# Value products of causal attention: one float32 matmul becomes three passes on high and low halves, two blocks late

## The chip, the cores and the metric

The kernel runs on one core of one Trainium2 chip. The metric is the device time of one execution in microseconds (us), smaller is better. The core has a matrix engine (TensorE, in the profile PE, its weight loads PEld), VectorE (DVE), ScalarE (ACT), GpSimd (POOL) and SyncE (SP), each with its own instruction queue worked off in order; they wait for each other on semaphores.

## The reference

The program is a two-layer network on an input `x` of 2 x 1024 x 256. Layer 0 is a Mamba block and a mixture of experts, layer 1 an attention with three heads over all tokens, then a causal attention, and a second mixture of experts. The change is in the causal attention, 16 query heads and 4 key heads of width 128:

```python
q = (x @ wq).reshape(b, s, H, HD)          # H = 16, KV = 4, HD = 128, s = 1024
k = (x @ wk).reshape(b, s, KV, HD)
v = (x @ wv).reshape(b, s, KV, HD)
q, k = apply_rope(q, cos, sin), apply_rope(k, cos, sin)
scores = jnp.einsum('bqhd,bkhd->bhqk', q, k) / np.sqrt(HD)
scores = jnp.where(causal[None, None], scores, jnp.finfo(scores.dtype).min)
probs = jax.nn.softmax(scores, axis=-1)
out = jnp.einsum('bhqk,bkhd->bqhd', probs, v).reshape(b, s, H * HD)
return out @ wo
```

## The kernel before

The causal attention is the function `attn2`. It works through eight units, `u` = 0 to 7: one key head of one batch with its `REP` = 4 query heads. In a unit the queries are cut into `TB` = 8 rows of blocks, 128 queries each, worked in descending order, row 7 first; row `i` has `i + 1` key blocks `j`. The function `schedule()` writes one list, `todo`, of tokens, and every engine goes through this list and does its part of each token, so the order of the tokens is the order in each queue:

- `score` (u, i, h): TensorE multiplies queries of row i and head h with the keys in three passes. Queries and keys are kept as a high half (rounded to the fast float32r format) and a low half (the rest), and `THREE` names the passes (high x high, high x low, low x high). VectorE takes the maximum (`reduce_max`, then `nb`), ScalarE the exponential, and the normalization by the reciprocal of the sum is GpSimd's for heads 0 to 2 and VectorE's for head 3 (`normal`).
- `turn` (u, i, j): TensorE transposes the four heads' probabilities of block j into one bank of its accumulation memory (PSUM), 4 or 5 in turn; ScalarE copies it into `eT`.
- `value` (u, i, j): TensorE adds `v[:, j]` times `eT` into the row's accumulator (bank 6 or 7), in float32. It comes one `turn` after its own.
- `out` (u, i): the finished row, copied by ScalarE into `ao`, is multiplied by `wo`; VectorE adds it to `hs`. It takes a bank of the same pair 4 and 5, and is put ahead of the second product of the next row.
- `project` (u, n), five in a unit for the next unit (the key and four heads): in row 4 before blocks 0, 2 and 4, in row 3 before block 2, in row 2 before block 1. TensorE makes it in 12 passes; VectorE applies the rotation (L1867 to L1869) and for the key subtracts its high half (L1873); GpSimd adds the parts (L1890) and makes the low half of the queries (L1895). The rotation of query head n waits for the low half of head n - 2.
- `values` (u): the projection of `v`, copied by ScalarE (L1976). In unit 0 `chores` puts the second batch's normalization on VectorE, one piece at each `turn`; unit 3 has four pieces more.

Scores, projections and `values` share banks 0 to 3 as they come (`unit_free` waits for whoever used the bank before); `turn` and `out` share banks 4 and 5 (`ring_free` waits for the entry before the last one).

Of the kernel before, what the change touches and what calls it, by code (L numbers as in the profile page):

```python
# [7 lines left out]
P = 128  # L8
F32 = mybir.dt.float32
# [1554 lines left out]
def attn2(nc, g, hs, norm_w, wq, wk, wv, wo):  # L1564
# [8 lines left out]
    with ctx:  # L1573
# [8 lines left out]
        WPIECE, WPIECES = 256, WC // 256  # L1582
        wo_s = sb("wo", [P, 2, REP, D])
        cos, sin = sb("cos", [P, L]), sb("sin", [P, L])
        mask_f, mask, ident_b = sb("mask_f", [P, P]), sb("mask", [P, P], BF16), sb("ident_b", [P, P], BF16)
        HI, LO = 0, 1
        ER = 4
        hT, wh, qT, kT = ([
            sb(n + half, shape, F32R) for half in ("hi", "lo")] for n, shape in (
            ("hT", [P, KC, L]), ("wh", [P, KC, WC]), ("qT", [P, REP, L]), ("kT", [P, L])))  # L1590
        v, eT = sb("v", [P, TB, HD]), sb("eT", [P, ER, REP * P])
        THREE = ((HI, HI), (HI, LO), (LO, HI))
        e = sb("e", [P, 2, REP, L])
        side = sb("side", [P, REP, 5 * P])
        ao = sb("ao", [P, 2, REP, P])
        mx, nb, sm, rc = (sb(n, [P, TB * REP]) for n in ("mx", "nb", "sm", "rc"))
        d_x = nc.dram_tensor("a2_dx", [B * L, D], F32, kind="Internal").ap()
        names = ("in", "own", "xn", "tr", "hT", "hlow", "whigh", "wlow", "cst", "unit", "w", "rot", "sum", "high", "rope", "rope_k",
                 "v", "nb", "e", "rc", "en", "en_last", "xout", "xin", "spare", "wo_in",
                 "tp", "eT", "o", "ao", "wo", "hs")  # L1600
        s = {n: sem(n) for n in names}
        block = ctx.enter_context(nc.Block())
        U = B * KV
# [21 lines left out]
        def schedule():  # L1625
# [9 lines left out]
            def turn(u, i, j):  # L1635
                put("turn", u, i, j)
                waiting.append((u, i, j))
                if len(waiting) > 1:
                    value(*waiting.pop(0))

            ahead = {7: [(p, 6, h) for h, p in enumerate((0, 1, 2, 3))] + [(p, 3, h) for h, p in enumerate((4, 5, 6, 7))],
# [71 lines left out]
        @block.sync  # L1713
        def _(sp):
            loads = [(nwb[:, :], norm_w.rearrange("(a n) -> a n", a=1).to_broadcast([P, D])),
                     (cos[:, :], g.d["cos"]), (sin[:, :], g.d["sin"]),
                     (mask_f[:, :], g.d["mask"])]
            sp.dma_start(d_x.rearrange("(j p) d -> p j d", p=P), x[:, :, :]).then_inc(s["xout"], 16)
            for u in range(U):
                kv = u % KV  # L1720
                if u > 0:
                    sp.wait_ge(s["wlow"], u * WPIECES)
                sp.dma_start(w_s[:, :, 0:REP * HD], wq.rearrange("(k p) n -> p k n", p=P)[:, :, kv * (REP * HD):(kv + 1) * (REP * HD)]).then_inc(s["w"], 16)
                sp.dma_start(w_s[:, :, REP * HD:(REP + 1) * HD], wk.rearrange("(k p) n -> p k n", p=P)[:, :, kv * HD:(kv + 1) * HD]).then_inc(s["w"], 16)
# [12 lines left out]

        @block.vector
        def _(dve):
# [59 lines left out]
            inverse(0, 2)  # L1799
            dve.wait_ge(s["in"], 64)  # L1800
            scaled(0, 0, TB)
            dve.tensor_copy(mask[:, :], mask_f[:, :])
            dve.tensor_copy(ident_b[:, :], ident[:, :]).then_inc(s["cst"], 1)

            def chores(u):
# [11 lines left out]
                    c += [lambda q=q: scaled(1, 2 * q, 2) for q in range(4)]  # L1817
                return c

            late, extra = [], []  # L1820

            def normal(u, i, h):
                q = i * REP + h
# [5 lines left out]
                    dve.tensor_scalar(probs(i, h), probs(i, h), rc[:, q:q + 1], None, ALU.mult).then_inc(s["en_last"], 1)  # L1829

            for what, u, i, h in todo:
                if what == "score":
                    n = unit[what, u, i, h]
                    q = i * REP + h
                    dve.wait_ge(s["unit"], done[what, u, i, h])
                    own(dve.reduce_max(mx[:, q:q + 1], pair(n, (i + 1) * P), AX_X))  # L1836
                    dve.tensor_scalar(nb[:, q:q + 1], mx[:, q:q + 1], -SCALE, None, ALU.mult).then_inc(s["nb"], 1)  # L1837
                    if late:
                        normal(*late.pop(0))
                    late.append((u, i, h))  # L1840
# [1 line left out]
                elif what == "turn":  # L1842
# [76 lines left out]
        def _(act):  # L1919
# [36 lines left out]
            for n, (what, u, i, h) in enumerate(todo):  # L1956
                if what == "turn":
                    k = turned[u, i, h]
                    act.wait_ge(s["tp"], k + 1)
                    act.activation(eT[:, k % ER, :], ps[:, bank[what, u, i, h], :], ACT.Copy).then_inc(s["eT"], 1)  # L1960
                    if u == 0 and (i, h) == (7, 5):
                        root(1, 3)
                    if u == 0 and (i, h) == (4, 3):
                        root(1, 4)
# [8 lines left out]
                    act.activation(hT[HI][:, int(i), :], pair(unit[what, u, i, h]), ACT.Copy).then_inc(s["hT"], 1)  # L1973
                elif what == "values":
                    act.wait_ge(s["unit"], done[what, u, i, h])
                    act.activation(flat(v[:, :, :]), pair(unit[what, u, i, h]), ACT.Copy).then_inc(s["v"], 1)  # L1976
# [14 lines left out]
        def _(pe):  # L1991
            pe.wait_ge(s["cst"], 1)

            def unit_free(token):

                for what, u, i, h in earlier[token]:
# [2 lines left out]
                    elif what == "project":  # L1999
                        pe.wait_ge(s["rot"], u * NPROJ + i + 1)  # L2000
                    elif what == "values":
                        pe.wait_ge(s["v"], u + 1)
                    else:
                        pe.wait_ge(s["hlow"], 2 * u + i + 1)

            def ring_free(t):

                r = ring_at[t]
                if r >= 2:
                    what, u, i, j = ring[r - 2]  # L2010
                    if what == "turn":
                        pe.wait_ge(s["eT"], turned[u, i, j] + 1)
                    else:
                        pe.wait_ge(s["hs"], outs[u, i] + 1)

            for token in todo:
# [53 lines left out]
                    tr.then_inc(s["tp"], 1)  # L2070
                elif what == "value":
                    k = turned[u, i, j]
                    pe.wait_ge(s["eT"], k + 1)
                    if j == 0:
                        if i == TB - 1:
                            pe.wait_ge(s["v"], u + 1)
                        if rows[u, i] > 1:
                            pe.wait_ge(s["ao"], rows[u, i] - 1)
                    mm = pe.matmul(ps[:, 6 + rows[u, i] % 2, :], v[:, j, :], eT[:, k % ER, :], start=(j == 0), stop=(j == i))  # L2079
                    if j == i:  # L2080
                        mm.then_inc(s["o"], 1)
                elif what == "out":
# [96 lines left out]
```

## Time and profile before

| | |
|---|---|
| median of 3 runs | 2725.68 us (2723.99 to 2726.79) |
| profiled execution | 2727.46 us, its span 2725.7 us |
| TensorE busy (PE) | 2422.0 us, 89% of the span |
| VectorE busy (DVE) | 1428.0 us, 52% |
| ScalarE busy (ACT) | 1131.9 us, 42% |
| GpSimd busy (POOL) | 1135.4 us, 42% |
| `attn2` | about 1484 to 2414 us of the span |

A busy share is an average over stages. What counts for the change is the stretch of `attn2`: which engine is full there, and where it waits. Matmuls overlap in the trace, since each is shown from its start to its last result; the distance between two starts tells what one occupies. A row of a timeline gives start, duration, engine, line, operation, and in brackets how long the engine had been idle and who ended it.

### The profile page before, as it was taken

What the parts mean: (1) busy time and instruction counts of PE and PEld (TensorE: products, weight loads), DVE (VectorE), ACT (ScalarE), POOL (GpSimd) and SP (SyncE); (2) the same over time, 40 slices, a digit from 0 to 9 for tenths busy, and PEclk for the clock granted to TensorE, in tenths of its full rate; (3) what the DMA queues carried; (4) which work ended last, traced back from release to release, by engine and by line L of the source; (5) the groups of instructions that cost most, each with busy time, mean ns of one, the idle gap of its engine ahead of it and who ended that gap; (6) DMA issues with size and microseconds to landing.
All of it is one profiled execution on the core that took longest, in us unless ns stands there. A gap on an engine that the chain in (4) does not pass through costs nothing. (4 is left out here: it accounts for less than half of the span.)

```text
span 2725.7 us, 34445 instructions
## 1 busy us (share of the span) xinstructions
PE 2422.0 (89%) x12334; PEld 1805.0 (66%) x12334; DVE 1428.0 (52%) x2528; ACT 1131.9 (42%) x1920; POOL 1135.4 (42%) x666
## 2 busy tenths in 40 slices
PE   6959999968999949969994799999999999968997
PEld 2349999946777638848862567776677776734554
DVE  6568888772222235434426575555555555453332
ACT  3557777621111124324421446455464554531221
POOL 0449999602333204322422454444444445303443
PEclk8969999989999969989986899999999999988999
DMA  6282351255112120000002000000000000036222
GB/s 236 86 318 56 132 233 63 86 163 186 32 32 33 27 95 1 1 1 1 1 1 88 1 12 20 9 12 8 13 20 9 12 8 18 15 102 190 45 45 61
DMA packets 107469, 168.22 MB, mean 62 GB/s; under 512 B 30468, under 2 KB 76166, under 8 KB 105096
## 3 DMA queue, kind: packets, MB, share of 16 engines
q1 hardware_dynamic: 92328, 145.22, 15.2%
q0 software_dynamic: 14976, 20.78, 4.6%
q8 instruction: 106, 1.74, 0.3%
q14 instruction: 59, 0.48, 0.1%
HBM read 115.81 MB, written 52.32 MB: 62 GB/s over the span
## 5 line engine op out<-in xcount | busy, mean ns | idle before, releaser
L670 POOL TENSOR_TENSOR mb_dbx<-mb_ud,mb_bb 128x1024 f32<-128x1024 f32 x128 | 302.0, 2363 | 58.1 <-DVE mb_h L528 42.4
L528 DVE TENSOR_TENSOR_SCAN mb_h<-ps,mb_dbx 128x1024 f32<-128x1024 f32 x128 | 292.2, 2289 | 49.5 <-ACT ps L640 42.2
L2079 PE MATMUL ps<-a_eT,a_v 128*128 128x512 f32 x576 | 298.3, 600 | 1.3 <-ACT a_eT L1960 1.3
L1908 POOL TENSOR_TENSOR a_e<-a_e,a_rc 128x1024 f32<-128x1024 f32 (+5 forms) x144 | 187.9, 1310 | 266.1 <-DVE a_rc L1826 265.7
L1836 DVE TENSOR_REDUCE a_mx<-ps 128x1 f32<-128x1024 f32 (+7 forms) x256 | 192.8, 753 | 199.8 <-PE ps L2060 199.4
L968 POOL DMA_INDIRECT e_acc<-e_hid,e_ids x78 | 123.6, 1585 | 371.4 <-DVE e_hid L1264 364.0
L1960 ACT ACTIVATE a_eT<-ps 128x512 f32<-128x512 f32 x288 | 171.1, 594 | 250.1 <-PE ps L2069 249.3
L772 PE MATMUL ps<-mb_dg,mb_hts 128*128 128x128 f32 x2048 | 251.9, 277 | 0.4
L772 PEld LDWEIGHTS ps<-mb_dg,mb_hts 128*128 128x128 f32 x2048 | 240.6, 193 | 1.9 <-issue 1.9
L1558 POOL TENSOR_TENSOR a_elo<-a_e,a_ehi 128x1024 fp32r<-128x1024 f32 x48 | 120.6, 2513 | 264.9 <-ACT a_ehi L1482 264.9
L2057 PE MATMUL ps<-a_kThi,a_qThi 128*128 128x512 f32 (+3 forms) x384 | 206.4, 537 | 21.6 <-DVE a_e L1869 9.8
L1250 DVE COPY e_work<-ps 128x256 f32<-128x256 f32 x78 | 33.1, 425 | 357.0 <-PE ps L1083 357.0
L1942 ACT ACTIVATE a_e<-ps,a_nb 128x1024 f32<-128x1024 f32 (+5 forms) x192 | 156.1, 813 | 87.2 <-DVE a_nb L1837 74.0
L1114 PE MATMUL ps<-e_wd,e_work 128*128 (+1 forms) x780 | 189.0, 384 | 1.9 <-ACT e_work L1013 1.9
L1095 PE MATMUL ps<-e_wg,e_work 128*128 x468 | 178.2, 518 | 5.0 <-DVE e_work L1250 1.4
L649 ACT ACTIVATE mb_hts<-ps 128x512 f32<-128x512 f32 x256 | 139.2, 595 | 95.2 <-PE ps L757 95.2
L1007 ACT ACTIVATE e_hid<-ps 128x688 f32<-128x688 f32 (+1 forms) x78 | 52.3, 670 | 300.6 <-PE ps L1095 300.6
L1095 PE MATMUL ps<-e_wu,e_work 128*128 x468 | 171.1, 502 | 0.0
L2069 PE MATMUL ps<-ident,a_e 128*128 128x128 f32 x992 | 151.3, 275 | 18.4 <-DVE hs L1883 16.0
L757 PE MATMUL ps<-ident,mb_h 128*128 128x128 f32 x1024 | 135.6, 276 | 32.9 <-DVE mb_h L528 32.8
L1114 PEld LDWEIGHTS ps<-e_wd,e_work 128*128 128x128 f32 (+1 forms) x780 | 138.9, 190 | 30.0 <-issue 15.7
L954 POOL DMA_INDIRECT e_xin<-e_rows,e_ids x78 | 77.0, 987 | 190.3 <-DVE e_ids L1239 166.6
(343 smaller groups left out, 5293.0 us busy)
## 6 DMA issues: line engine op xcount, KB each, us to landing
mb_bb<-mb_db_rows SPq DMA_DIRECT2D x16, 1024.0 KB, 12.8
mb_ddiag<-mb_dg SPq DMA_DIRECT2D x1, 8192.0 KB, 22.3
mb_dg<-mb_ddiag SPq DMA_DIRECT2D x8, 1024.0 KB, 14.4
e_wg<-in_g SPq DMA_DIRECT2D x8, 688.0 KB, 10.4
e_wu<-in_u SPq DMA_DIRECT2D x8, 688.0 KB, 11.1
e_wd<-in_d SPq DMA_DIRECT2D x8, 640.0 KB, 10.6
mb_dxa<-mb_bb SPq DMA_DIRECT2D x8, 512.0 KB, 2.6
mb_dz<-mb_xz SPq DMA_DIRECT2D x8, 512.0 KB, 2.9
```

The costliest lines, as they stand in the source:

```text
L528: dve.tensor_tensor_scan(h[:, at % 2, :], pair(at % 2), dbx[:, at % 2, :], 0.0, ALU.mult, ALU.add).then_inc(s_h, 1)
L670: pool.tensor_tensor(dbx[:, at % 2, :], ud[:, kk % 2, 0, :], bb[:, n, :], ALU.mult).then_inc(s_dbx, 1)
L772: mm = pe.matmul(ps[:, 6 + half, q * P:(q + 1) * P], hts[:, at % 2, c:c + P], dg[:, n, c:c + P], start=(n == 0 and q == 0), stop=(n == NS ...
L1095: mm = pe.matmul(ps[:, b0 + a, 0:FN], xT[:, i % 2, k * P:(k + 1) * P], w[:, ds(e), k, a * FN:(a + 1) * FN].rearrange("p a n -> p (a n)"), ...
L1114: mm = pe.matmul(ps[:, 6, 0:D], hT[0:n, i % 2, c * P:(c + 1) * P], wd[0:n, ds(e), c, :].rearrange("p a n -> p (a n)"), start=(c == 0), sto ...
L1836: own(dve.reduce_max(mx[:, q:q + 1], pair(n, (i + 1) * P), AX_X))
L1908: pool.tensor_tensor(probs(i, h), probs(i, h), rc[:, q:q + 1].to_broadcast([P, (i + 1) * P]), ALU.mult).then_inc(s["en"], 1)
L1942: act.activation(probs(i, h), pair(n, (i + 1) * P), ACT.Exp, bias=nb[:, q:q + 1], scale=SCALE, accum_out=sm[:, q:q + 1]).then_inc(s["e"], 1)
L1960: act.activation(eT[:, k % ER, :], ps[:, bank[what, u, i, h], :], ACT.Copy).then_inc(s["eT"], 1)
L2057: mm = pe.matmul(ps[:, o + t, 0:c1 - c0], qT[x_][:, j, i * P:(i + 1) * P], kT[y_][:, c0:c1], start=(x_ == y_), stop=(x_ == LO and not last))
L2069: tr = pe.transpose(ps[:, bank[token], h * P:(h + 1) * P], probs(i, h, j * P, (j + 1) * P), ident[:, :])
L2079: mm = pe.matmul(ps[:, 6 + rows[u, i] % 2, :], v[:, j, :], eT[:, k % ER, :], start=(j == 0), stop=(j == i))
```

## The change

The value product is made like the scores, in three passes on high and low halves of `v` and of `eT`. ScalarE's copies now write the high halves `eT[HI]` and `v[HI]` in float32r; VectorE subtracts them from what stands in PSUM and writes the low halves. For `eT` that is the new function `low`, done as VectorE's first work of the token that follows the `turn`. Semaphores `eTlow` and `vlow` take the place of `eT` and `v` where TensorE waits: for a value product, and for the reuse of a bank. The product stands two turns behind its own instead of one. To make room `eT` has three slots instead of four, `mask_f` lies in `side`, and `mx` keeps two rows' worth.

```diff
-        ER = 4
+        ER = 3
-        v, eT = sb("v", [P, TB, HD]), sb("eT", [P, ER, REP * P])
+        v, eT = ([sb(n + half, shape, F32R) for half in ("hi", "lo")] for n, shape in (("v", [P, TB, HD]), ("eT", [P, ER, REP * P])))
...
+        mask_f = side[:, 0, 0:P]
...
-        mx, nb, sm, rc = (sb(n, [P, TB * REP]) for n in ("mx", "nb", "sm", "rc"))
+        nb, sm, rc = (sb(n, [P, TB * REP]) for n in ("nb", "sm", "rc"))
+        mx = sb("mx", [P, 2 * REP])
...
-                if len(waiting) > 1:
+                if len(waiting) > 2:
                     value(*waiting.pop(0))
...
+            def low(u, i, j):
+                k = turned[u, i, j]
+                dve.wait_ge(s["eT"], k + 1)
+                dve.tensor_tensor(eT[LO][:, k % ER, :], ps[:, bank["turn", u, i, j], :], eT[HI][:, k % ER, :].bitcast(F32),
+                                  ALU.subtract).then_inc(s["eTlow"], 1)
...
             for what, u, i, h in todo:
+                if turned_low:
+                    low(*turned_low.pop(0))
...
                         normal(*late.pop(0))
+                    turned_low.append((u, i, h))
                     if extra:
                         extra.pop(0)()
+                elif what == "values":
+                    dve.wait_ge(s["v"], u + 1)
+                    dve.tensor_tensor(flat(v[LO][:, :, :]), pair(unit[what, u, i, h]), flat(v[HI][:, :, :]).bitcast(F32), ALU.subtract).then_inc(s["vlow"], 1)
...
-                    act.activation(eT[:, k % ER, :], ps[:, bank[what, u, i, h], :], ACT.Copy).then_inc(s["eT"], 1)
+                    act.activation(eT[HI][:, k % ER, :], ps[:, bank[what, u, i, h], :], ACT.Copy).then_inc(s["eT"], 1)
...
                     elif what == "values":
-                        pe.wait_ge(s["v"], u + 1)
+                        pe.wait_ge(s["vlow"], u + 1)
...
                     if what == "turn":
-                        pe.wait_ge(s["eT"], turned[u, i, j] + 1)
+                        pe.wait_ge(s["eTlow"], turned[u, i, j] + 1)
...
-                    pe.wait_ge(s["eT"], k + 1)
+                    pe.wait_ge(s["eTlow"], k + 1)
                     if j == 0:
                         if i == TB - 1:
-                            pe.wait_ge(s["v"], u + 1)
+                            pe.wait_ge(s["vlow"], u + 1)
...
-                    mm = pe.matmul(ps[:, 6 + rows[u, i] % 2, :], v[:, j, :], eT[:, k % ER, :], start=(j == 0), stop=(j == i))
+                    for x_, y_ in THREE:
+                        mm = pe.matmul(ps[:, 6 + rows[u, i] % 2, :], v[x_][:, j, :], eT[y_][:, k % ER, :], start=(j == 0 and x_ == y_), stop=(j == i and x_ == LO))
```

The order of the tokens changes with the lag. Around the projections of a unit (T a `turn`, V a `value`, both with row and block):

```
before: PROJ0 T40 V55 T41 V40 PROJ1 T42 OUT5 V41 T43 V42 PROJ2 T44 V43 T30 V44 T31 V30 PROJ3 T32 OUT4 V31 T33 V32 T20 V33 PROJ4 T21 V20 T22 OUT3 V21 S70 T10 V22 S71 T11 V10 S72 T00 OUT2 V11 S73 OUT1 V00
after:  PROJ0 T40 V54 T41 V55 PROJ1 T42 V40 T43 OUT5 V41 PROJ2 T44 V42 T30 V43 T31 V44 PROJ3 T32 V30 T33 OUT4 V31 T20 V32 PROJ4 T21 V33 T22 V20 S70 T10 OUT3 V21 S71 T11 V22 S72 T00 V10 S73 OUT2 V11 OUT1 V00
```

## Rows read from the trace of the kernel before

**Rows 1.** Windows, unit 2: us, busy us (x instructions) of PE PEld DVE ACT POOL, PEclk

```profile
1755.00:1869.00 114.00, 111.53 (x573) 81.88 (x572) 60.50 (x129) 58.22 (x118) 53.62 (x36) 0.99 0.04 12
```

**Rows 2.** Groups of `attn2`: busy us, mean ns, then idle time before them

```profile
L2079 PE MATMUL ps<-a_eT,a_v 128*128 128x512 f32 x576 | 298.3, 600 | 1.3 <-ACT a_eT L1960 1.3
...
L1883 DVE TENSOR_TENSOR hs<-ps,hs 128x256 f32<-128x256 f32 x63 | 26.6, 422 | 48.0 <-PE ps L2088 47.5
...
L1877 DVE TENSOR_TENSOR a_hTlo<-ps,a_hThi 128x1024 fp32r<-128x1024 f32 x2 | 2.4, 1224 | 4.2 <-ACT a_hThi L1973 4.2
```

**Rows 3.** Timeline of PE, unit 2: projection 2, passes 2 and 12, then turn, value, turn

```profile
1827.14 0.39 PE L2036 MATMUL ps<-a_hTlo,a_whhi 128*128 128x512 f32 x1
...
1829.43 0.39 PE L2036 MATMUL ps<-a_hThi,a_whlo 128*128 128x512 f32 x1
1829.67 0.60 PE L2069 MATMUL ps<-ident,a_e 128*128 128x128 f32 x4
1830.10 1.02 PE L2079 MATMUL ps<-a_eT,a_v 128*128 128x512 f32 x2
1830.96 0.60 PE L2069 MATMUL ps<-ident,a_side 128*128 128x128 f32 x4
```

**Rows 4.** Timeline of ACT, unit 2: the eviction of that turn

```profile
1830.30 0.60 ACT L1960 ACTIVATE a_eT<-ps 128x512 f32<-128x512 f32 x1 [3.46 <-PE ps L2069]
```

**Rows 5.** Timeline of DVE, unit 2: the key's subtraction, rotation 2, rotation 3

```profile
1826.51 1.23 DVE L1873 TENSOR_TENSOR a_kTlo<-x,a_kThi 128x1024 fp32r<-128x1024 f32 x1
...
1829.87 1.23 DVE L1867 TENSOR_TENSOR x<-ps,a_cos 128x1024 f32<-128x1024 f32 x1 [1.79 <-PE ps L2036]
...
1832.34 1.22 DVE L1869 TENSOR_TENSOR x<-ps,a_sin 64x1024 f32<-64x1024 f32 x1
1838.47 1.23 DVE L1867 TENSOR_TENSOR x<-ps,a_cos 128x1024 f32<-128x1024 f32 x1 [4.91 <-POOL a_qTlo L1895]
```

**Rows 6.** Timeline of PE, unit 2: `out` of row 4, and the stall before T21

```profile
1836.77 1.89 PE L2088 MATMUL ps<-a_wo,a_ao 128*128 128x256 f32 x8
1838.50 1.02 PE L2079 MATMUL ps<-a_eT,a_v 128*128 128x512 f32 x2
...
1842.77 0.96 PE L2069 MATMUL ps<-ident,a_e 128*128 128x128 f32 x4 [1.96 <-DVE hs L1883]
```

**Rows 7.** Timeline of ACT: the eviction of `v` in units 1, 2 and 3

```profile
1648.33 1.03 ACT L1976 ACTIVATE a_v<-ps 128x1024 f32<-128x1024 f32 x1 [4.71 <-PE ps L2044]
...
1759.96 1.03 ACT L1976 ACTIVATE a_v<-ps 128x1024 f32<-128x1024 f32 x1 [4.71 <-PE ps L2044]
...
1873.25 1.03 ACT L1976 ACTIVATE a_v<-ps 128x1024 f32<-128x1024 f32 x1 [4.71 <-PE ps L2044]
```

**Rows 8.** Timeline of PE: unit 1's stall before T21; `out` of row 1, unit 7

```profile
1731.14 0.63 PE L2069 MATMUL ps<-ident,a_e 128*128 128x128 f32 x4 [1.96 <-DVE hs L1883]
...
2407.58 1.99 PE L2088 MATMUL ps<-a_wo,a_ao 128*128 128x256 f32 x8 [0.69 <-ACT a_ao L1981]
```

**Rows 9.** Windows of rows 7 to 5, unit 2 and unit 0, columns as in rows 1

```profile
1759.85:1817.26 57.41, 57.41 (x310) 42.09 (x310) 31.52 (x94) 36.55 (x83) 25.75 (x24) 1.00 0.07 24
...
1528.00:1590.10 62.10, 57.78 (x299) 41.34 (x298) 48.99 (x135) 38.05 (x86) 28.66 (x24) 0.97 0.05 14
```

**Rows 10.** Timeline of DVE, unit 0: variance chain to the `hs` add, inverse to rotation 3

```profile
1600.55 2.36 DVE L1750 TENSOR_TENSOR a_a_n_mean<-a_a_n_st 128x8 f32<-128x8 f32 x1
...
1604.46 0.42 DVE L1883 TENSOR_TENSOR hs<-ps,hs 128x256 f32<-128x256 f32 x1
...
1608.51 0.20 DVE L1764 RECIPROCAL a_a_n_rstd<-a_a_n_sd 128x8 f32<-128x8 f32 x1
...
1613.94 1.23 DVE L1867 TENSOR_TENSOR x<-ps,a_cos 128x1024 f32<-128x1024 f32 x1 [0.22 <-DVE a_a_n_rstd L1768]
```

**Rows 11.** Window of unit 3's rows 7 to 5: us, DVE busy (x instructions), PEclk

```profile
1873.00:1930.50 57.50, 38.86 (x102) 1.00 0.08 24
```

**Rows 12.** Window of 4 us behind unit 2's stall, columns as in rows 1

```profile
1844.00:1848.00 4.00, 4.00 (x12) 2.60 (x11) 0.00 (x0) 1.91 (x3) 2.93 (x2) 0.71 0.00 0
```

More of the change, by code:

```diff
@@ L1584, in attn2 @@
         cos, sin = sb("cos", [P, L]), sb("sin", [P, L])
-        mask_f, mask, ident_b = sb("mask_f", [P, P]), sb("mask", [P, P], BF16), sb("ident_b", [P, P], BF16)
+        mask, ident_b = sb("mask", [P, P], BF16), sb("ident_b", [P, P], BF16)
         HI, LO = 0, 1
-        ER = 4
+        ER = 3
         hT, wh, qT, kT = ([
@@ L1594, in attn2 @@
         side = sb("side", [P, REP, 5 * P])
+        mask_f = side[:, 0, 0:P]
         ao = sb("ao", [P, 2, REP, P])
-        mx, nb, sm, rc = (sb(n, [P, TB * REP]) for n in ("mx", "nb", "sm", "rc"))
+        nb, sm, rc = (sb(n, [P, TB * REP]) for n in ("nb", "sm", "rc"))
+        mx = sb("mx", [P, 2 * REP])
         d_x = nc.dram_tensor("a2_dx", [B * L, D], F32, kind="Internal").ap()
         names = ("in", "own", "xn", "tr", "hT", "hlow", "whigh", "wlow", "cst", "unit", "w", "rot", "sum", "high", "rope", "rope_k",
-                 "v", "nb", "e", "rc", "en", "en_last", "xout", "xin", "spare", "wo_in",
-                 "tp", "eT", "o", "ao", "wo", "hs")
+                 "v", "vlow", "nb", "e", "rc", "en", "en_last", "xout", "xin", "spare", "wo_in",
+                 "tp", "eT", "eTlow", "o", "ao", "wo", "hs")
         s = {n: sem(n) for n in names}
@@ L1716, in _ @@
                      (cos[:, :], g.d["cos"]), (sin[:, :], g.d["sin"]),
-                     (mask_f[:, :], g.d["mask"])]
+                     (mask_f, g.d["mask"])]
             sp.dma_start(d_x.rearrange("(j p) d -> p j d", p=P), x[:, :, :]).then_inc(s["xout"], 16)
@@ L1801, in _ @@
             scaled(0, 0, TB)
-            dve.tensor_copy(mask[:, :], mask_f[:, :])
+            dve.tensor_copy(mask[:, :], mask_f)
             dve.tensor_copy(ident_b[:, :], ident[:, :]).then_inc(s["cst"], 1)
@@ L1818, in chores @@
                 return c
-            late, extra = [], []
+            late, extra, turned_low = [], [], []
+            def low(u, i, j):
[3 more added lines that the diff above has]
+                                  ALU.subtract).then_inc(s["eTlow"], 1)
             def normal(u, i, h):
@@ L1835, in _ @@
                     dve.wait_ge(s["unit"], done[what, u, i, h])
-                    own(dve.reduce_max(mx[:, q:q + 1], pair(n, (i + 1) * P), AX_X))
-                    dve.tensor_scalar(nb[:, q:q + 1], mx[:, q:q + 1], -SCALE, None, ALU.mult).then_inc(s["nb"], 1)
+                    top = mx[:, q % (2 * REP):q % (2 * REP) + 1]
+                    own(dve.reduce_max(top, pair(n, (i + 1) * P), AX_X))
+                    dve.tensor_scalar(nb[:, q:q + 1], top, -SCALE, None, ALU.mult).then_inc(s["nb"], 1)
                     if late:
@@ L1975, in _ @@
                     act.wait_ge(s["unit"], done[what, u, i, h])
-                    act.activation(flat(v[:, :, :]), pair(unit[what, u, i, h]), ACT.Copy).then_inc(s["v"], 1)
+                    act.activation(flat(v[HI][:, :, :]), pair(unit[what, u, i, h]), ACT.Copy).then_inc(s["v"], 1)
                 elif what == "value" and h == i:
```

## The prediction

> **What bounds the kernel now.** I read the page first: TensorE is busy for most of the span, and the chain that ended last stays in the final expert stage, which the diff does not touch. So I cut the trace by windows to `attn2` (1484 to 2414 us). A unit (one key head of one batch) shows TensorE busy 111.5 of 114 us at full clock, VectorE 60.5 [rows 1]. The groups of the stage give the prices [rows 2]; timelines of the engines over one unit give the order and the few places where TensorE waits.
>
> Is TensorE really full, or are its busy times only overlapping? In the timeline ten three-pass matmuls of 512 columns start 2.29 us apart in all, 0.229 each, with nothing between them [rows 3]. It is full, and in this stage a shorter matmul shortens the kernel, unless somebody makes TensorE wait. (The Trainium skill, "Perfetto Trace Analysis", section "Identifying the Most-Contended Engine", says that busy matmuls mislead and weight-load time tells the headroom. By that rule TensorE, with 81.9 us of weight loads in 114 [rows 1], is a quarter idle, and the shorter products would save up to nothing. The starts in rows 3 speak against it.)
>
> **Removed.** A value product is one float32 matmul, traced as two instructions [rows 2]. From its start to the next transpose it occupies 1830.96 - 1830.10 = 0.86 us [rows 3]. Three passes cost 3 x 0.229 = 0.69. Saved: 288 x 0.17 = **-49.0 us** (the ends: nothing, if the three passes together cost what the float32 product did; -61, if a pass costs 0.216 as an instruction of `out` does, eight in 1.73 us, below).
>
> **Added.** The evictions on ScalarE keep shape and price. VectorE gets 288 subtractions of 512 columns from PSUM, unseen before. The nearest rows, also from PSUM, are 256 columns at 0.42 and 1024 at 1.224 us [rows 2]; 512 columns lie on their line at 0.69. I take 0.69 and keep 0.42 and 1.22 as ends. And 8 subtractions of `v`, 1.22 each. Per unit that is 36 x 0.69 + 1.2 = 26 us on VectorE, which then has 87 of about 108. It is not the bound by its sum. What counts is its order: it works down one list, and now TensorE may not reuse a transpose bank (`ring_free`), nor start a value product, before VectorE has passed that transpose.
>
> **How late.** A transpose group starts at 1829.67 [rows 3], its eviction at 1830.30 for 0.60 [rows 4]; so the low half can start 0.63 + 0.60 + 0.03 = 1.26 us after the transposes start and ends 1.95 after. In rows 7 to 5 a step with one score takes TensorE 2.25 to 2.45 us and VectorE about 2.0 to 2.2: hidden. The trouble is the stretch where the next unit's projections stand between the turns. Each gives VectorE a rotation, which starts 0.20 after the projection's last slot (1829.87 after 1829.67) and takes 3.69 (1829.87 to 1833.56), for the key 1.23 more (`kTlo`); and projection 3's rotation waits for GpSimd until 4.91 after the one before [rows 5]. With only two banks, the third ring entry behind each projection needs the low half that stands behind the rotation.
>
> I walked one unit. Zero is the end of projection 0; transposes 0.43, products 0.69, projection 12 x 0.23 = 2.76, `out` 1.73 (1836.77 to 1838.50 [rows 6]):
> - Rotation 0 runs 0.2 to 3.9, the lows of T40, T41 to 5.3, rotation 1 with `kTlo` 5.3 to 10.3. TensorE: T40, T41 and two products to 2.2, projection 1 to 5.0, T42, one product, T43 to 6.5. `out` of row 5 needs T42's bank: low at 11.0. **Stall 4.5.**
> - `out`, product, projection 2 to 16.2, T44, T30 and products to 18.4. T31 needs T44's low behind rotation 2 (16.4 to 20.1): 20.9. **Stall 2.5.**
> - Projection 3 ends 24.8, T32, T33 to 26.3. Rotation 3 runs 25.0 to 28.7 (GpSimd frees it at 20.1 + 4.9). `out` of row 4 needs T32's low: 29.5. **Stall 3.2.**
> - Projection 4 ends 35.8, rotation 4 39.7, T10 starts at 40.5 instead of 39.4, `out` of row 3 at 41.15. **Stall 1.3.**
>
> Together 11.4 us. Before, this stretch has one stall, 2.1 us before 1842.77, behind an `hs` add that stands after a rotation that waits for GpSimd [rows 6]; the walk contains its cause. Net 9.3 a unit, 7 units with projections: **+65.1**.
>
> **Unit borders.** `v` is evicted from 1759.96 for 1.03 [rows 7]; its banks now come free 1.2 later, and the row-7 reduction of the first score stands behind that subtraction. Walked: score 1 waits 0.9, score 2 another 0.8, less 0.1 of slack: 1.6 x 8 = **+12.8**. Two blocks late, row 1's last product now stands directly ahead of row 1's `out`, which needs the eviction of it: the last unit shows that wait, 0.69 before 2407.58 plus a weight load [rows 8], I take 0.84 x 7 = **+5.9**. In the last unit there are no scores between the turns, and three `out`s come 0.5 early for their bank: **+1.5**.
>
> **Units with chores.** Unit 0 carries the second batch's norm on VectorE. There rows 7 to 5 take 62.1 us with VectorE busy 49.0; unit 2 has 57.4 and 31.5 [rows 9]. With 21 x 0.69 + 1.2 = 15.7 more and some 5 us of its idle time left, unit 0 is VectorE's: 70 us, +8 where TensorE alone would have won 3.6: 11.6 worse than the sum so far. In its projections the variance chain (1600.55 to 1604.46) comes before T42's low and the inverse (1608.51 to 1613.94, less 0.2) before T44's [rows 10]: 9.1, less 2.1 that such a stall costs it already: 7.0. Together about +18. Unit 3, with 38.9 busy in the same 57.5 [rows 11], comes to 54.6 and its gaps, about 60 for 55.3: +4.7. **+22.7.**
>
> **The clock.** In 4 us behind the 2 us stall of unit 2 the granted clock was 0.71, so part at the lower of the two levels [rows 12]. Unit 2 lasts 113.29 (1759.96 to 1873.25), unit 1, whose equal stall at 1731.14 [rows 8] kept full clock, 111.63 (1648.33 to 1759.96) [rows 7]: a drop costs 1.66. Three of eight such stalls of about 2 us had one. I count 4.5 us as a sure drop, 3.2 as 0.8, 2.5 as 0.5: 2.3 drops x 1.66 x 7 = 27, less 5 that three drops cost now: **+22**. (The Trainium skill, "TensorE: Matmul & The Clock Gate", part 1, says that idleness throttles the array and activity frees it; rows 12 agree, though not every such stall did it. By the rule taken strictly each of the three long stalls costs a drop, 30 instead of 22.)
>
> **Sum.** -49.0 + 65.1 + 12.8 + 5.9 + 1.5 + 22.7 + 22 = +81. The profiled execution took 2727.46 (span 2725.7, 1.8 around it), so 2808; the median of the runs is 2725.68, 1.8 lower. Forecast **2806 us**, 3.0% slower.
>
> **Free by the diff:** `mask_f` inside `side`, the smaller `mx`, ER = 3 (a slot's product stands ahead of the turn that rewrites it). [...]
>
> **Rivals.**
> 1. *The queue coupling is slight* (faster). VectorE's sum fits beside TensorE's. If the stalls in the projection stretch summed to no more than about 4 us a unit, against 2.1 now, the 49 us would win: (4 - 2.1) x 7 + 12.8 + 7.4 - 49 = -15.5, with few drops about 2710; with no coupling at all 2677. It decides at 4.3 us of new net stall a unit, drops included. Against it: 3.69 us of rotation stand in one piece ahead of each low [rows 5], and TensorE has only 1.6 to 2.3 us of work to its third ring entry. Chance 0.12.
> 2. *Stalls as walked, but without drops of the clock and with chores absorbed*: +36 or so, 2762. For it: five of eight 2 us stalls kept the clock. Chance 0.25.
> 3. *Gain and loss balance*, within 0.2%: 0.04.
> 4. *VectorE saturates*: at 1.22 a subtraction 19 us more a unit, 2900 and above; also if SBUF traffic with GpSimd stretches it. The rotations, of the same kind from PSUM, keep 1.22 beside GpSimd's adds. Chance 0.07.
> 5. The forecast: 0.52, own range 2780 to 2830.
>
> **Numbers.** 0.2% (5.5 us) is about what a measurement here can tell from no change. 80% range 2735 to 2840: rival 1, most of 3 and most of 4 stay outside. Faster 0.12, same 0.04, slower 0.84.
>
> **What would show it.** Value products as three starts 0.23 apart, two blocks behind their turn; `eTlo` at 0.69 mean, 288 times; TensorE waiting for `eTlo` (line of the subtraction) some 11 us a unit, longest 4 to 5 us before an `out` right after projection 1; full-clock share lower in the projection stretches; units 1 to 6 near 120 us instead of 112 to 116; unit 0 near 145; unit 7 shorter by 3. Wrong if `eTlo` costs otherwise, if TensorE's waits on it stay below 4 us a unit, or if the granted clock stays at 1.00.

## The result and the profile after

The changed kernel takes 2832.53 us (median of 4 runs, 2829.47 to 2838.2), the kernel before 2725.56 beside it: ratio 1.0395, 95% interval 1.0375 to 1.0415. It is 107 us slower by the medians, 102 by the spans of the two profiled executions (2827.6 against 2725.7).

First the groups of `attn2` after the change, columns as in [rows 2].

```profile
L1827 DVE TENSOR_TENSOR a_eTlo<-ps,a_eThi 128x512 fp32r<-128x512 f32 x288 | 193.7, 683 | 48.7 <-ACT a_eThi L1975 45.7 <-DVE a_a_n_rstd L1770 0.2
L2104 PE MATMUL ps<-a_wo,a_ao 128*128 128x256 f32 x512 | 146.7, 437 | 77.8 <-DVE a_eTlo L1827 63.7 <-ACT a_ao L1996 14.1
...
L1866 DVE TENSOR_TENSOR a_vlo<-ps,a_vhi 128x1024 fp32r<-128x1024 f32 x8 | 9.8, 1225 | 45.9 <-ACT a_vhi L1991 45.9
```

The new subtraction costs the 0.69 that was forecast. In the second row 63.7 us of TensorE's idle time stand ahead of `out` alone, ended by VectorE's subtraction. Over the whole stage TensorE waits 96.1 us for `eTlo`, 40 times; before, it waited for no such thing.

The timeline of TensorE over unit 1, from T42 on; a bracket is idle time and who ended it.

```profile
1741.79 0.60 PE L2084 MATMUL ps<-ident,a_e 128*128 128x128 f32 x4
1742.14 0.49 PE L2095 MATMUL ps<-a_eThi,a_vhi 128*128 128x512 f32 x1
1742.47 0.39 PE L2095 MATMUL ps<-a_eTlo,a_vhi 128*128 128x512 f32 x1
1742.70 0.39 PE L2095 MATMUL ps<-a_eThi,a_vlo 128*128 128x512 f32 x1
1742.93 0.60 PE L2084 MATMUL ps<-ident,a_e 128*128 128x128 f32 x4
...
1747.69 3.56 PE L2104 MATMUL ps<-a_wo,a_ao 128*128 128x256 f32 x8 [4.16 <-DVE a_eTlo L1827]
1759.21 0.66 PE L2084 MATMUL ps<-ident,a_side 128*128 128x128 f32 x4 [2.24 <-DVE a_eTlo L1827]
1767.94 3.65 PE L2104 MATMUL ps<-a_wo,a_ao 128*128 128x256 f32 x8 [3.04 <-DVE a_eTlo L1827]
1780.74 0.63 PE L2084 MATMUL ps<-ident,a_e 128*128 128x128 f32 x4 [0.86 <-DVE a_eTlo L1827]
...
1796.04 1.99 PE L2104 MATMUL ps<-a_wo,a_ao 128*128 128x256 f32 x8 [1.98 <-ACT a_ao L1996]
```

Transposes to transposes, with a product between, are now 1742.93 - 1741.79 = 1.14 us against 1.29 [rows 3]. Then come the four stalls of the walk, where before there was one of 1.96 [rows 6, 8]. The fifth bracket is the `out` of row 1. And see the duration of the two `out`s behind the long stalls: 3.56 and 3.65 against 1.89 [rows 6].

VectorE in the same stretch shows why T42's bank comes free so late.

```profile
1741.99 1.23 DVE L1882 TENSOR_TENSOR x<-ps,a_cos 128x1024 f32<-128x1024 f32 x1
1743.23 1.23 DVE L1883 TENSOR_TENSOR x<-ps,a_sin 64x1024 f32<-64x1024 f32 x1
1744.47 1.22 DVE L1884 TENSOR_TENSOR x<-ps,a_sin 64x1024 f32<-64x1024 f32 x1
1745.72 1.23 DVE L1888 TENSOR_TENSOR a_kTlo<-x,a_kThi 128x1024 fp32r<-128x1024 f32 x1
1746.86 1.28 DVE L1827 TENSOR_TENSOR a_eTlo<-ps,a_eThi 128x512 fp32r<-128x512 f32 x2
```

T42 is transposed at 1741.79; its low half stands behind four operations without a gap, first of the two that end at 1748.1.

Windows: unit 0, unit 1, the last unit, and 4 us behind the first and the third stall; columns as in [rows 1].

```profile
1531.00:1682.20 151.20, 115.51 (x594) 92.44 (x593) 107.78 (x224) 62.11 (x123) 56.10 (x36) 0.90 0.02 6
1682.20:1804.06 121.86, 108.00 (x601) 89.10 (x601) 81.06 (x165) 57.30 (x117) 53.51 (x36) 0.97 0.04 12
2428.86:2515.40 86.54, 81.28 (x472) 67.10 (x471) 56.00 (x137) 46.82 (x101) 21.88 (x21) 1.00 0.00 1
1749.00:1753.00 4.00, 4.00 (x15) 3.16 (x15) 0.42 (x1) 0.00 (x0) 0.15 (x1) 0.76 0.00 0
1770.00:1774.00 4.00, 4.00 (x18) 3.21 (x18) 1.04 (x2) 1.25 (x2) 1.81 (x1) 0.82 0.00 0
```

In unit 1 no engine is full: VectorE has 81 us of work in 122. Units 0 to 6 last 151.1, 121.9, 123.6, 132.5, 123.5, 121.9, 123.3 (eviction of `v` to the next one), against 120.6, 111.6, 113.3, 116.1, 111.6, 113.3, 111.6 before; the last takes 86.8 to the end of its last `hs` add (the window above stops 0.3 short of it) against 87.7. The lower clock shows most in unit 0, from its first projection to the next eviction of `v`:

```profile
1595.96:1682.20 86.24, 62.48 (x289) 49.79 (x288) 50.36 (x78) 25.72 (x42) 29.40 (x14) 0.84 0.00 0
```

The same stretch before the change:

```profile
1586.98:1648.33 61.35, 55.25 (x271) 40.51 (x270) 40.31 (x59) 25.94 (x43) 29.64 (x14) 1.00 0.00 1
```

### The profile page after: what moved, and what is told of

It reads as the page before. It is cut to its first block and busy times, and to the rows that moved or that the text cites. A ratio compares the mean times of both kernels' runs of the same rounds, so it can differ in the third digit from the quotient of the medians.

```text
span 2827.6 us, 35317 instructions
## 1 busy us (share of the span) xinstructions
PE 2419.7 (86%) x12622; PEld 1877.8 (66%) x12622; DVE 1600.2 (57%) x2824; ACT 1127.9 (40%) x1920; POOL 1134.8 (40%) x666
## 5 line engine op out<-in xcount | busy, mean ns | idle before, releaser
L1923 POOL TENSOR_TENSOR a_e<-a_e,a_rc 128x1024 f32<-128x1024 f32 (+5 forms) x144 | 188.5, 1311 | 270.3 <-DVE a_rc L1834 269.3
L1975 ACT ACTIVATE a_eThi<-ps 128x512 fp32r<-128x512 f32 x288 | 171.2, 594 | 284.3 <-PE ps L2084 284.1
L1827 DVE TENSOR_TENSOR a_eTlo<-ps,a_eThi 128x512 fp32r<-128x512 f32 x288 | 193.7, 683 | 48.7 <-ACT a_eThi L1975 45.7
L2104 PE MATMUL ps<-a_wo,a_ao 128*128 128x256 f32 x512 | 146.7, 437 | 77.8 <-DVE a_eTlo L1827 63.7
L1905 POOL TENSOR_TENSOR x<-x 128x1024 f32<-128x1024 f32 x35 | 90.0, 2573 | 219.4 <-DVE x L1884 219.4
L2104 PEld LDWEIGHTS ps<-a_wo,a_ao 128*128 128x128 f32 x512 | 105.1, 215 | 102.1 <-issue 69.1
L2072 PE MATMUL ps<-a_kThi,a_qThi 128*128 128x512 f32 (+3 forms) x384 | 141.6, 369 | 33.4 <-ACT a_e L1957 11.2
L2084 PE MATMUL ps<-ident,a_e 128*128 128x128 f32 x992 | 151.6, 276 | 14.6 <-DVE a_eTlo L1827 11.4
## 6 DMA issues: line engine op xcount, KB each, us to landing
mb_dg<-mb_ddiag SPq DMA_DIRECT2D x8, 1024.0 KB, 13.5
e_wu<-in_u SPq DMA_DIRECT2D x8, 688.0 KB, 10.5
```

What stands on the lines that cost most here:

```text
L1827: dve.tensor_tensor(eT[LO][:, k % ER, :], ps[:, bank["turn", u, i, j], :], eT[HI][:, k % ER, :].bitcast(F32), ALU.subtract).then_inc(s["eT ...
L1923: pool.tensor_tensor(probs(i, h), probs(i, h), rc[:, q:q + 1].to_broadcast([P, (i + 1) * P]), ALU.mult).then_inc(s["en"], 1)
L1975: act.activation(eT[HI][:, k % ER, :], ps[:, bank[what, u, i, h], :], ACT.Copy).then_inc(s["eT"], 1)
L2084: tr = pe.transpose(ps[:, bank[token], h * P:(h + 1) * P], probs(i, h, j * P, (j + 1) * P), ident[:, :])
L2104: mm = pe.matmul(ps[:, bank[token], 0:D], ao[:, rows[u, i] % 2, h, :], wo_s[:, u % 2, h, :], start=(h == 0), stop=(h == REP - 1))
```

## Experiments

Ratios are to the kernel before, which ran beside each on the same chip; 0.1% is 2.7 us.

**One part alone: the three passes, without low halves on VectorE.** The product runs in three passes on the high half of `eT`, waits for ScalarE's copy and is two blocks late; the low halves of the probabilities are left out.

```diff
-                    pe.wait_ge(s["eTlow"], k + 1)
+                    pe.wait_ge(s["eT"], k + 1)
-                        mm = pe.matmul(ps[:, 6 + rows[u, i] % 2, :], v[x_][:, j, :], eT[y_][:, k % ER, :], start=(j == 0 and x_ == y_), stop=(j == i and x_ == LO))
+                        mm = pe.matmul(ps[:, 6 + rows[u, i] % 2, :], v[x_][:, j, :], eT[HI][:, k % ER, :], start=(j == 0 and x_ == y_), stop=(j == i and x_ == LO))
```

> The changed kernel without any subtraction for the low half of the probabilities: three passes that take the high half each time (the low half is left out of the result), waits on ScalarE's copy as before, v in halves with its subtraction and waits, two blocks late. It prices what remains: -49 for the passes, +13 for v, +6 for the last out of a unit: 2696 us. If the passes save less than thought, nearer 2726; a rival that sees three passes as dear as one product expects 2745.

Measured: 2713.08, ratio 0.9942 (0.9921 to 0.9962). The gain is there, 16 us of the forecast 30. The five ordinary units are 2.4 us shorter in the mean, where 36 x 0.15 = 5.4 are saved; in unit 1 the wait for the `hs` add (1.96) is gone, one of 2.06 for ScalarE's copy stands near it, and 0.71 for another copy, 0.91 for `ao`, 0.59 for `vlo` and 0.31 for an exponential are new; all its waits sum to 4.6 where they were 2.5.

```profile
1741.32 0.92 PE L2081 MATMUL ps<-ident,a_e 128*128 128x128 f32 x4 [2.06 <-ACT a_eThi L1972]
```

As a limit, with two passes (the low half of the probabilities left out) and one block late:

> No low half of the probabilities (left out of the result), v in halves, two passes (high and low of v with the high half of the probabilities), one block late as before. Saves 288 x (0.86 - 0.46) = 115, pays 13 for v and nothing for the last out: 2624 us. If VectorE, ScalarE or GpSimd become the bound first, up to 2660.

Measured: 2667.92, ratio 0.978 (0.9738 to 0.9822): 60 of the 102 us. In this stage part of what TensorE saves comes back as waits: the stall behind the `hs` add grew from 1.96 to 3.33, all the waits of unit 1 from 2.5 to 5.5. The rest of the difference was not traced.

**The other way: the old product in the changed kernel,** one float32 matmul on the high halves, so that the low halves are made but not used.

> The changed kernel with its subtractions, waits and lag, but the value product is one float32 matmul again, on the high halves (low halves left out of the result). The three passes should save 0.17 us each time except where a stall hides them, about 7 of 36 in a unit: 288 x 0.17 less 8, so 41 us slower than the changed kernel, 2873 us, whichever theory of the stalls holds. Rival (three passes cost as much as one float32 product): no difference, 2832.

Measured: 2857.13, ratio 1.0451 (1.043 to 1.0472), 15 us above the changed kernel by the ratios, 32 by the two spans; the units sum to 24 more. The passes are worth less than the 43 us of their occupation here, since a longer product fills part of the stalls: the five ordinary units are 3.8 us longer in the mean, not 5.4, and the waits of unit 1 sum to 12.4 instead of 13.9.

**VectorE's amount of work, with nobody waiting for it.** The kernel before, with 288 extra operations at the place of `low`, each behind the same wait for `eT`; its result is untouched.

```diff
+                if turned_low:
+                    idle_low(*turned_low.pop(0))
...
+                dve.tensor_tensor(scratch[:, k % 4, :], cos[:, 0:REP * P], sin[:, 0:REP * P], ALU.subtract)
```

> The kernel before, with 288 additional VectorE subtractions of 512 columns on idle data, each in the place where the change has its low half and behind the same wait for ScalarE's copy, but nobody waits for them; the result is untouched. Theory (the wait on them costs, not their time): near the kernel before, at most 25 us more, most of that in unit 0, where VectorE is full, so 2730 to 2750. Rival (the load on VectorE costs): at least 80 us more, above 2805.

Measured: 2806.13, ratio 1.0268 (1.0244 to 1.0292). A miss, and the groups say why: the subtraction took 1212 ns, not 683. Nobody waited for it, yet it was no stand-in for `low`. The same with a maximum over 512 columns, one tensor in:

> As e3_unwaited_work, but the idle work is a maximum over 512 columns of one SBUF tensor, so one input and about 0.68 us like the change's own subtraction, in place of a subtraction of two SBUF tensors that came out at 1.21 us and slowed GpSimd's work too. The result is untouched. Theory (order and waits of the ring): at most 25 us above the kernel before. Theory of load: 60 us or more above it, as e3_unwaited_work had 73.

Measured: 2750.0, ratio 1.0082 (1.0055 to 1.011), at 680 ns a time. This is the load of the 288 operations alone (without the 8 subtractions of `v`): about 22 us, 11 of them in unit 0 (131.8 us), 0.9 in the mean of the ordinary units. A window one unit long shows what that settles:

```profile
1753.00:1867.00 114.00, 110.91 (x566) 81.28 (x566) 81.06 (x165) 57.32 (x117) 53.96 (x37) 0.99 0.04 12
```

VectorE is busy 81.06 us, to the hundredth what it is in unit 1 of the changed kernel, and units 1 and 2 take 113.9 and 113.8 instead of 121.9 and 123.6. VectorE's amount is not what costs the 107 us.

**The bank made free earlier, by ScalarE's copy.** The low half is made from SBUF (high minus high, so that the low half of the probabilities is left out); everything else is as changed.

```diff
-                dve.tensor_tensor(eT[LO][:, k % ER, :], ps[:, bank["turn", u, i, j], :], eT[HI][:, k % ER, :].bitcast(F32),
+                dve.tensor_tensor(eT[LO][:, k % ER, :], eT[HI][:, k % ER, :].bitcast(F32), eT[HI][:, k % ER, :].bitcast(F32),
...
-                        pe.wait_ge(s["eTlow"], turned[u, i, j] + 1)
+                        pe.wait_ge(s["eT"], turned[u, i, j] + 1)
```

> The changed kernel, but the low half is made from the copy in SBUF (high half less itself, so the low half of the probabilities is left out of the result), and a bank of the ring comes free with ScalarE's copy as before; the value product still waits for the subtraction, VectorE does as many subtractions in the same order. Theory (TensorE waits for the reuse of a bank, behind a rotation in VectorE's list): the four stalls after the projections vanish, 9 us a unit and the clock drops that they cause, so about 2745 us, the waits ahead of v and of the last out of a unit stay. Rival (the product's own wait for its low half, or VectorE's load by itself, is what costs): within 15 us of the changed kernel, 2815 to 2835.

Measured: 2826.45, ratio 1.0356 (1.0331 to 1.038). A miss by 80 us. The same fault as above, here in a timeline of VectorE and one of GpSimd:

```profile
1769.39 2.88 DVE L1827 TENSOR_TENSOR a_eTlo<-a_eThi 128x512 fp32r<-128x512 f32 x1
1772.20 0.41 DVE L1898 TENSOR_TENSOR hs<-ps,hs 128x256 f32<-128x256 f32 x1
1772.53 2.55 DVE L1827 TENSOR_TENSOR a_eTlo<-a_eThi 128x512 fp32r<-128x512 f32 x1
```

```profile
1768.83 2.89 POOL L1905 TENSOR_TENSOR x<-x 128x1024 f32<-128x1024 f32 x1 [4.23 <-DVE x L1884]
1771.68 2.85 POOL L1910 TENSOR_TENSOR a_qTlo<-x,a_qThi 128x1024 fp32r<-128x1024 f32 x1
```

VectorE's subtraction ends 0.55 us after GpSimd's operation does, both times (1772.27 after 1771.72, 1775.08 after 1774.53): these subtractions, with two inputs in SBUF, end as if they had waited for GpSimd to finish, and so do 54 of the 67 shown singly that took 0.89 us or more, 0.54 to 0.56 behind a GpSimd operation's end. Its mean is 1179 ns, and now the product waited for it, in unit 1 for 3.15 us before 1754.34 and three times more, 6.4 in all. So a third version, with a maximum over the high half (679 ns) in place of the subtraction, the product still waiting for VectorE, and the high half in all three passes:

> As e1_bank_free, but VectorE's work in the place of the low half is a maximum over the high half in SBUF (about 0.68 us instead of 1.18), and the product takes the high half of the probabilities in all three passes, so their low half is left out of the result. A bank comes free with ScalarE's copy, the product waits for VectorE. Theory (reuse of a bank costs): stalls after the projections gone, 2745 to 2765. Rival (VectorE's load or the product's wait): 2810 or more.

Measured: 2746.52, ratio 1.0061 (1.0043 to 1.0079), as expected. Its waits in unit 1's projection stretch:

```profile
1742.60 0.73 PE L2097 MATMUL ps<-a_eThi,a_vhi 128*128 128x512 f32 x2 [1.80 <-DVE a_scratch L1830]
...
1751.21 0.73 PE L2097 MATMUL ps<-a_eThi,a_vhi 128*128 128x512 f32 x2 [0.48 <-DVE a_scratch L1830]
```

2.3 us in place of 10.3. With VectorE's work in the same place of its list, the product two blocks late waits little; it was the bank.

**The bank wait taken away with all of the work kept.** Three banks for transposes and `out` (4 to 6), one accumulator (7): the entry that must wait for a `low` is the fourth, not the third.

```diff
-        bank = {t: (4, 5)[r % 2] for t, r in ring_at.items()}
+        bank = {t: (4, 5, 6)[r % 3] for t, r in ring_at.items()}
...
-                if r >= 2:
-                    what, u, i, j = ring[r - 2]
+                if r >= 3:
+                    what, u, i, j = ring[r - 3]
...
-                        if rows[u, i] > 1:
-                            pe.wait_ge(s["ao"], rows[u, i] - 1)
+                        if rows[u, i] > 0:
+                            pe.wait_ge(s["ao"], rows[u, i])
```

> The changed kernel with all its work, but turn and out go round three banks of PSUM instead of two, the third taken from the rows' accumulator, which has one bank instead of two, so a row's first product waits until ScalarE has copied the row before. Theory (the third ring entry behind a projection has to wait, a fourth need not): walked as in the prediction, the stall of 4.2 us before the out of row 5 vanishes, 2.3 us remain as the wait of a product for its low half behind rotation 2, 1.1 at T20; 7.5 us a unit and most drops of the clock less, 53 + 22 us, so about 2757 us (ratio to the kernel before 1.012). Rival (it is the latency of the low half, not the number of banks): within 15 us of the changed kernel.

Measured: 2755.95, ratio 1.0089 (1.0062 to 1.0117). A hit: 3.06% of the 3.95% are gone. Unit 1 takes 112.16 us. Its waits from projection 1 on, but for one of 0.69 for a score:

```profile
1739.34 0.50 PE L2095 MATMUL ps<-a_eThi,a_vhi 128*128 128x512 f32 x1 [1.80 <-DVE a_eTlo L1827]
1744.46 1.89 PE L2104 MATMUL ps<-a_wo,a_ao 128*128 128x256 f32 x8
1748.04 0.63 PE L2084 MATMUL ps<-ident,a_e 128*128 128x128 f32 x4 [0.98 <-DVE a_eTlo L1827]
1754.02 0.47 PE L2095 MATMUL ps<-a_eThi,a_vhi 128*128 128x512 f32 x1 [0.34 <-ACT a_ao L1996]
...
1771.41 1.99 PE L2104 MATMUL ps<-a_wo,a_ao 128*128 128x256 f32 x8 [1.73 <-ACT a_ao L1996]
```

In this unit no wait of over 2 us is left, its granted clock is 1.00 (0.97 after the change), and `out` is back at 1.89: the clock term went with the stalls. The ordinary units take 112.4 in the mean, as before the change (112.3). What is left stands in the units with chores: unit 0 takes 138.3, with stalls of 3.82 and 5.17, and unit 3 122.2.

**VectorE's order instead of the banks.** In units 1 to 7 the rotation's three or four operations are issued one by one, each followed by a `low` that is due; all of the work is kept.

```diff
                 if turned_low:
                     low(*turned_low.pop(0))
+                    if pieces:
+                        pieces.pop(0)()
...
+                    pieces += [p_cos, p_lo, p_hi] + ([p_key] if i == 1 else [])
```

> The changed kernel with all its work, only VectorE's list in another order: the three pieces of a rotation (and the key's subtraction) of units 1 to 7 no longer stand together ahead of the low halves, one piece follows each low half, the rest ahead of the next projection or score. Theory (order, not amount): stall before the out of row 5 falls from 4.2 to about 0.7 us, that at T31 to nearly nothing, that before the out of row 4 moves to a wait of about 1 us; 2750 us. Rival (VectorE has too much work, whatever its order): no more than 15 us better than the changed kernel.

Measured: 2802.75, ratio 1.0268 (1.025 to 1.0285): 35 us off by the ratios, not 80. VectorE's timeline shows where the wait went:

```profile
1748.36 0.69 DVE L1827 TENSOR_TENSOR a_eTlo<-ps,a_eThi 128x512 fp32r<-128x512 f32 x1 [3.84 <-ACT a_eThi L1996]
...
1760.66 0.69 DVE L1827 TENSOR_TENSOR a_eTlo<-ps,a_eThi 128x512 fp32r<-128x512 f32 x1 [4.08 <-ACT a_eThi L1996]
```

VectorE now idles for ScalarE's eviction. In ScalarE's list the high half of the rotated query stands ahead of it and waits for GpSimd's add, which waits for the last piece of the rotation, now later. This chain is read from the code and the trace, it was not tried by itself. A wait in one ordered list had moved to another.

**One block late** in the changed kernel, as before the change.

> The changed kernel with its products one block late instead of two, nothing else. Turns without a score between them take TensorE 1.57 us from a turn's start to the next product, a low half is ready after 1.95 to 2.05, so 0.5 us more at some ten steps of a unit; the wait before the last out of a unit (2 us) goes. Theory: 5 to 25 us above the changed kernel. Rival (the second block of lag is itself a cost): faster than the changed kernel.

Measured: 2871.22, ratio 1.0517 (1.048 to 1.0555), 33 us above the changed kernel, more than I gave it; TensorE waits 134.7 us for `eTlo`, 82 times. The second block of delay is worth its place.

**Chores after `low`.** The extra pieces of units 0 and 3 one behind each `low`, not ahead of it.

```diff
                 if turned_low:
                     low(*turned_low.pop(0))
+                    if extra:
+                        extra.pop(0)()
...
                     turned_low.append((u, i, h))
-                    if extra:
-                        extra.pop(0)()
```

> The changed kernel with VectorE's chores of units 0 and 3 (normalization of the second batch) done behind the low half of their turn instead of ahead of it, same amount of work. Theory: the waits of 8.7 and 7.5 us in unit 0's projections lose the variance chain and the inverse, 9 us, and the drops of the clock shorten: 8 to 15 us below the changed kernel, all in unit 0. Rival (amount, not order): no difference.

Measured: 2818.88, ratio 1.0322 (1.0286 to 1.0358), 20 us less by the ratios. Unit 0 fell from 151.1 to 141.5; its two long stalls from 8.74 and 7.50 to 5.54 and 2.24.

```profile
1608.87 3.67 PE L2104 MATMUL ps<-a_wo,a_ao 128*128 128x256 f32 x8 [5.54 <-DVE a_eTlo L1827]
1620.51 0.66 PE L2084 MATMUL ps<-ident,a_side 128*128 128x128 f32 x4 [2.24 <-DVE a_eTlo L1827]
```

The other units together are 2 longer, so the units show 8 of the 20. Another 5 stand ahead of the first unit (its eviction of `v` comes at 1525.97 instead of 1531.06), where the code is the same, and I can't place the rest.

**All that helped, together.** Three banks, chores after `low`, and at the end of a unit:

```diff
                 if u + 1 < U:
+                    value(*waiting.pop(0))
                     put("score", u + 1, 7, 3)
```

> The changed kernel, all of its work, with three edits together: three ring banks and one accumulator bank (alone: 2755.95, ratio 1.0089), VectorE's chores one piece after each low half instead of ahead of it (alone on the changed kernel: 20 us off, from 151.1 to 141.5 in unit 0 and 132.5 to 132.9 in unit 3), and at the end of each unit the product of row 1 and the out of row 2 put ahead of the last score, so that the score covers the copy that the out of row 1 waits for (row-1 wait 1.72 us a unit in the run with three banks). My theory: what the banks left is VectorE's order in unit 0 and one wait at each unit's end. Unit 0 gives 5 to 9 us (its ring stalls are gone already with three banks, so less than the 20), each of units 0 to 6 gives 1.5 at its end (10 us in all), so about 2739, ratio 1.005 (1.002 to 1.008), the row-1 wait below 0.5, ordinary units near 110.6. Rival, VectorE's amount: with 108 us of work in it unit 0 keeps its length whatever the order, and the end of a unit gives back its wait at the next unit's first scores: 2750 to 2756, units still 112.2. In neither case is it faster than the kernel before by more than 0.2%.

Measured: 2736.36 (median of 12), ratio 1.0024 (1.001 to 1.0037). The evictions of `v` at the ends of units 0 and 1 (the first is at 1533.30):

```profile
1665.63 1.03 ACT L1992 ACTIVATE a_vhi<-ps 128x1024 fp32r<-128x1024 f32 x1 [4.65 <-PE ps L2060]
1775.73 1.03 ACT L1992 ACTIVATE a_vhi<-ps 128x1024 fp32r<-128x1024 f32 x1 [4.65 <-PE ps L2060]
```

Ordinary units take 110.1 to 111.3 us, 1.7 in the mean less than before the change: there the passes win. Unit 0 takes 132.3 (before 120.6), unit 3 119.0 (116.1), and that loses it again. Unit 0 has 108.1 us of VectorE work in 132.3. No version with all of the work beat the kernel before.

## Why the prediction was right

Forecast 2806, measured 2832.53: inside the 80% range of 2735 to 2840, but 2.5 us outside the forecast's own range of 2780 to 2830. The mechanism is the one forecast; the size came out a quarter too small, 81 us for 107. By its steps:

- **Removed.** 1.14 instead of 1.29 from turn to turn: 288 x 0.15 = 43 us, forecast 49. The first of a product's three passes is followed only after 0.33 us (1742.47 - 1742.14), not 0.229, so a product occupies 0.79, not 0.69; the transposes ahead of it gave back 0.08.
- **Price of a subtraction.** 683 ns, forecast 0.69; `vlo` 1225, forecast 1.22. The line through the two PSUM rows held. (The Trainium skill, "VectorE: DVE Perf Modes", section "The TRN2 errata — SBUF-src ops pay a fixed extra latency per instruction", gives a float32 tensor_tensor add of 512 columns as 691 ns measured; the subtraction here, with one input in PSUM, is 1.2% below it.) VectorE's work in an ordinary unit came to 81, forecast 87.
- **The walk.** Stalls of 4.5, 2.5, 3.2, 1.3 forecast, 4.16, 2.24, 3.04, 0.86 measured: 10.3 for 11.4, each at its place. (The four forecast stalls add to 11.5.)
- **Unit borders.** The two scores at a unit's head wait 0.60 and 0.31, forecast 0.9 and 0.8. The `out` of row 1 waits 1.98, forecast 0.84, the wait furthest off in an ordinary unit. I had taken the copy's own delay; but in ScalarE's list it stands behind the exponential of the next unit's score 3, whose maximum on VectorE stands behind a `low` (0.67) and, ahead of that, a reciprocal that waited 1.27 for the exponential of score 2. The last experiment puts the product and an `out` ahead of that score, that wait is gone, and an ordinary unit is 1.8 us shorter in the mean than in the run with three banks.
- **Units with chores.** Unit 0: forecast +26.8, measured +30.5; unit 3: +13.5 and +16.4. The unit 0 stalls stand where they were put. But two errors partly cancel there: rows 7 to 5, up to the first projection, grew by 5.6 us (59.3 to 64.9), forecast 8, and the stretch behind them by 24.9 (61.35 to 86.24). Its waits grew by 17.7 (6.1 to 23.8) and its 15 products gave back 2.3, which leaves some 9 us at the clock of 0.84; the prediction gave unit 0 no more for the clock than the others, 3. One timeline, of unit 0 after the change:

```profile
1615.51 3.75 PE L2104 MATMUL ps<-a_wo,a_ao 128*128 128x256 f32 x8 [8.74 <-DVE a_eTlo L1827]
1633.47 1.12 PE L2084 MATMUL ps<-ident,a_side 128*128 128x128 f32 x4 [7.50 <-DVE a_eTlo L1827]
```

- **The clock.** In unit 1 two `out`s run 1.67 and 1.76 us longer behind their stalls, 3.4 in all, forecast 2.3 x 1.66 = 3.8. All 15 stalls of over 3 us ahead of an `out` were followed by a slow one; behind the middle stall of 2.24 the transposes took the usual 0.65 to 0.66 in five of six units. The granted clock is 0.97 in unit 1, 0.90 in unit 0.
- **Last unit.** Forecast 3.0 shorter, measured 0.9: three `out`s wait 0.42 each, forecast 0.5, and one transpose group 1.53, forecast nothing.

The spans differ by 21 us more than the sum said. An ordinary unit was forecast at -6.1 + 9.3 + 1.6 + 0.8 + 3.1 = 8.8 more and took 10.5: 5 x 1.7. In its terms: the products gave 5.4 for 6.1; the waits grew by 11.4 (2.5 to 13.9 in unit 1) for 11.7, a sum that is right in part by luck, since the `out` of row 1 was put too low and the walk and the scores too high; what remains, 4.5 for 3.1, is the clock and what no wait shows. Unit 0 adds 3.7, unit 3 2.9, the last unit 2.1. The last 3.3 stand ahead of the first unit: its eviction of `v` comes at 1531.06 instead of 1527.71. In the experiments, with the same code up to there, it came between 1524.73 and 1534.89, so I put no step to it.

Rival 1 (slight coupling) fails by the count: 10.3 us of stalls against its 4. Rival 2 (no drops of the clock, chores absorbed) fails by the clock of 0.97 in unit 1 and by unit 0's 30.5 us. Rival 4 (contention with GpSimd) was not this kernel's case, but it is real: two experiments met it. The causes are shown by runs: of 107 us, about 83 are the reuse of a bank behind VectorE's list (three banks alone take them off, clock drops included; the bank made free early takes off 91, with a stand-in for the subtraction); about 22 would be the added load where nobody waits for it; the passes by themselves give back 16. These shares are from different runs and overlap, so they need not sum to the result.

## What to carry to other kernels

Before work is given to an engine with room in its sum, look at what will wait for it and what stands ahead of it in its list: here the same 81 us of VectorE work cost an ordinary unit 0.9 us with nobody waiting, and 10.5 with a PSUM bank behind it, the passes' saving already taken off. Walk the few steps around the largest block in that list by hand, counting how many ring entries the producer has in hand; one more bank took off 83 us, the split rotation 35 and the later chores 20. Then ask of each cure which ordered list gets the wait next.

## What was not expected of the hardware

A VectorE subtraction with both inputs in SBUF took 1179 and 1212 ns in the mean for 512 columns where one from PSUM and SBUF took 683 and a maximum with one SBUF input 680. Of some 210 shown singly in the first of these runs, some 145 took 0.67 to 0.70 and 67 took 0.89 to 2.89. GpSimd suffered too: its normalization went from 1311 to 1518 ns, its add from 2573 to 2957. (The Trainium skill, "SBUF — State Buffer", section "SBUF: two separate sides", says that a VectorE operation with two SBUF inputs and a GpSimd operation that reads SBUF share ports under an exclusive lock, and the later one waits for the whole of the other. The 54 ends of 0.54 to 0.56 us after GpSimd's agree with it.) Whoever wants VectorE's load as a stand-in must keep its operand places too.

Stalls of over 3 us were paid twice: the eight matmuls of `out` took 2.53 to 3.75 us behind all 15 stalls of 3.02 to 8.74 ahead of them, 1.89 with none. Nearer to 2 us it went either way: `out` kept 1.97 behind a stall of 2.94 and 1.99 behind four waits of 1.98 or 1.99 for `ao`, but took 3.57 and 3.60 behind two more of 1.99.

```profile
1568.25 1.97 PE L2104 MATMUL ps<-a_wo,a_ao 128*128 128x256 f32 x8 [2.94 <-DVE a_eTlo L1827]
...
1940.82 2.53 PE L2104 MATMUL ps<-a_wo,a_ao 128*128 128x256 f32 x8 [3.49 <-DVE a_eTlo L1827]
...
2173.96 3.60 PE L2104 MATMUL ps<-a_wo,a_ao 128*128 128x256 f32 x8 [1.99 <-ACT a_ao L1996]
```

Behind a wait of 1.80 in unit 1 of the run with three banks the granted clock stayed at 1.00, and `out` kept 1.89.
